# A macaron of two feed-forward blocks, attention and experts on one core: norms by half, an earlier table request, keys turned first

## What is computed

```python
x = x + 0.5 * _L0_ffn_ref(_layernorm(x), ...)   # step 1
x = x + _L0_attn_ref(_layernorm(x), ...)
x = x + 0.5 * _L0_ffn_ref(_layernorm(x), ...)   # step 3
x = x + 0.5 * experts(...); x = x + linear_attention(...); x = x + 0.5 * experts(...)

def _layer(x, wqkv, qs, ksc, wo, lg, lb, w1, b1, w2, b2):   # _L0_ffn_ref runs two of these
    q, k, v = split(shift_token(x) @ wqkv)          # 8 heads of 64
    q = q / clip(norm(q), 1e-12) * qs               # the same for k
    q, k = rotary_xpos(q, k)                        # q*cos*scale + rotate_half(q)*sin*scale; k with 1/scale
    x = x + local_attention(q, k, v) @ wo           # windows of 64, this one and the one before
    h = layernorm(shift_token(x)) * lg + lb
    a, g = split(h @ w1 + b1)                       # 341 each
    return x + (a * gelu(g)) @ w2 + b2
```

## Time and profile before

| | us |
|---|---|
| median of 3 executions | 2468.88 (2466.38 to 2472.57) |
| the profiled execution, its own time | 2465.03 |
| its span, first to last instruction | 2462.9 |
| PE, DVE, ACT, POOL busy | 2116.9, 1809.3, 1462.6, 1058.3 |
| mean granted TensorE clock | 0.946 of full speed |

### The profile page before, as it was taken

One profiled execution on the slowest core, in us unless ns is written; L12 is line 12 of the kernel. 1 busy time (PEld: TensorE's weight loads), 2 busy tenths in 40 slices (PEclk: granted clock), 3 DMA queues, 4 the chain that ended last, 5 costly groups with the idle time before them and its releaser, 6 DMA issues. The chain is left out here.

```text
span 2462.9 us, 56322 instructions
## 1 busy us (share of the span) xinstructions
PE 2116.9 (86%) x23398; PEld 1565.7 (64%) x23398; DVE 1809.3 (73%) x2815; ACT 1462.6 (59%) x2389; POOL 1058.3 (43%) x800
## 2 busy tenths in 40 slices
PE   2799999998989868999868999999989997597968
PEld 1566666666666645555536667676666664495758
DVE  3688888888888646777727888888888884563556
ACT  0477776766666515666546776766666674363635
POOL 4665555545555210000035565655555450550245
PEclk8799999999999968999979999999999998698979
DMA  7000000079999995000000000000000003121122
GB/s 151 1 2 1 2 2 2 1 78 105 111 137 129 126 127 51 2 2 2 2 1 1 2 2 2 2 2 2 2 2 2 1 2 76 54 66 37 35 75 80
DMA packets 211376, 90.91 MB, mean 37 GB/s; under 512 B 79700, under 2 KB 206721, under 8 KB 210996
## 3 DMA queue, kind: packets, MB, share of 16 engines
q1 hardware_dynamic: 202596, 72.27, 24.5%
q0 software_dynamic: 6080, 11.76, 1.5%
q10 hardware_dynamic: 2448, 3.28, 0.6%
HBM read 24.31 MB, written 63.41 MB: 36 GB/s over the span
## 5 line engine op out<-in xcount | busy, mean ns | idle before, releaser
L490 POOL TENSOR_TENSOR work<-work,rot_tables 128x512 f32<-128x512 f32 x256 | 382.6, 1515 | 317.3 <-ACT work L594 317.3
L498 POOL TENSOR_TENSOR work<-work 128x1024 f32<-128x1024 f32 x128 | 304.8, 2381 | 283.6 <-DVE work L924 278.4
L941 DVE TENSOR_TENSOR work<-work,small 128x1024 f32<-128x1024 f32 x128 | 234.4, 1833 | 56.6 <-ACT small L608 50.1
L924 DVE TENSOR_TENSOR work<-work,rot_tables 128x1024 f32<-128x1024 f32 x128 | 219.3, 1713 | 11.6 <-ACT work L594 11.6
L1081 DVE TENSOR_REDUCE small<-psum 128x4 f32<-128x1024 f32 x128 | 156.6, 1223 | 90.3 <-PE psum L1582 88.5
L1482 PE MATMUL psum<-centered,ffn_w 128*128 128x256 f32 x768 | 191.2, 401 | 3.0 <-DVE centered L985 2.9
L705 ACT ACTIVATE work<-psum 128x1024 f32<-128x1024 f32 x128 | 131.0, 1024 | 88.7 <-PE psum L1582 88.4
L1323 PE MATMUL psum<-qkv_w_hi,h_hi 128*128 128x512 f32 x384 | 180.0, 469 | 2.2 <-ACT work L594 2.2
L1420 PE MATMUL psum<-work 64*128 64x128 f32 (+1 forms) x2048 | 178.9, 304 | 0.0
L1482 PEld LDWEIGHTS psum<-centered,ffn_w 128*128 128x128 f32 x768 | 146.0, 197 | 31.2 <-DVE centered L985 4.4
L1453 PE MATMUL psum<-work,v 128*32 128x192 f32 (+1 forms) x4096 | 164.8, 302 | 0.0
(11 more groups left out here) (279 smaller groups left out, 5266.1 us busy)
## 6 DMA issues: line engine op xcount, KB each, us to landing
h_area<-mean_weights SPq DMA_DIRECT2D x24, 2048.0 KB
tile_x<-h_area SPq DMA_DIRECT2D x39, 128.5 KB, 2.1
stage<-in_consts ACTq DMA_DIRECT2D x1, 2817.0 KB, 12.0
tile_x<-h_area SPq DMA_DIRECT2D x39, 64.5 KB, 1.8
work<-in_x SPq DMA_DIRECT2D x4, 512.0 KB, 27.2
expert_w<-in_ew SPq DMA_DIRECT2D x1, 2048.0 KB, 8.4
expert_w<-in_ew SPq DMA_DIRECT2D x8, 256.0 KB, 6.6
work<-y_tokens SPq DMA_DIRECT2D x4, 512.0 KB, 6.1
```

What stands on the lines that cost most here:

```text
L490: last = pool.tensor_tensor(b[:, :, :, o_], a[:, :, :, i_], tab[:, l, 1, t, :, o_].unsqueeze(2).to_broadcast([P, 2, HEADS, 32]), ALU.mult)
L498: pool.tensor_tensor(rC[:, t, :], rC[:, t, :], rB[:, t, :], ALU.add).then_inc(f_sum, 1)
L924: dve.tensor_tensor(g(rC[:, t, :]), g(rA[:, t, :]), tab[:, l, 0, t, :, :].unsqueeze(2).to_broadcast([P, 2, HEADS, DH]), ALU.mult)\
L941: dve.tensor_tensor(c_, c_, sm[0][:, 96 + 16 * t:112 + 16 * t].unsqueeze(2).to_broadcast([P, 16, DH]), ALU.mult).then_inc(f_nrm, 1)
```

## The change

1. GpSimd's `rotated` becomes two instructions of 512 columns.
2. `clip`, `rnorm` are done for each tile by itself (16 columns each), and `qk_norm(i, 0)` waits only for tile 0's root.
3. On ACT the GELU table is asked for right behind `rstd`; `rnorm(i, 0)` comes behind `gelu`, then the exponentials, then `x_square` and `rnorm(i, 1)`.
4. On DVE `clip(i, 0)` comes behind `sums(i, 0)`, then `gated`, and only then `cosines(i, 1)`, `qk_norm(i, 0)`, `x_center`, `sums(i, 1)`, `clip(i, 1)`, `resid2`, `qk_norm(i, 1)`.
5. On PE the keys of both tiles are turned before any query; the wait for `o_norm` stands behind the keys.

```diff
                 def rotated(i, t):
...
-                    pool.tensor_tensor(rC[:, t, :], rC[:, t, :], rB[:, t, :], ALU.add).then_inc(f_sum, 1)
+                    for h in range(2):
+                        n_ = slice(h * INNER, (h + 1) * INNER)
+                        last = pool.tensor_tensor(rC[:, t, n_], rC[:, t, n_], rB[:, t, n_], ALU.add)
+                    last.then_inc(f_sum, 1)
...
-                def rnorm(i):
-                    act.wait_ge(f_ssm, i + 1)
-                    link(act.activation(sm[0][:, 64:96], sm[0][:, 32:64], ACT.Ln, scale=65536.0))
-                    act.activation(sm[0][:, 96:128], sm[0][:, 64:96], ACT.Exp, scale=-0.5, bias=half_ln[:, 0:1])\
-                        .then_inc(f_rn, 1)
+                def rnorm(i, t):
+                    part_ = lambda a: sm[0][:, a + 16 * t:a + 16 * t + 16]
+                    act.wait_ge(f_ssm, 2 * i + t + 1)
+                    link(act.activation(part_(64), part_(32), ACT.Ln, scale=65536.0))
+                    act.activation(part_(96), part_(64), ACT.Exp, scale=-0.5, bias=half_ln[:, 0:1]).then_inc(f_rn, 1)
...
                     if old:
                         square(i - 2)
                         rstd(i - 2)
+                        act.preload_act_table_set(GELU_SET)
...
                     if old:
                         gelu(i - 2)
+                    if new:
+                        rnorm(i, 0)
+                    if mid:
+                        for q in range(3):
+                            exps(i - 1, q)
                     if pre:
                         x_square(n)
                     if new:
-                        rnorm(i)
-                    if mid:
-                        for q in range(3):
-                            exps(i - 1, q)
+                        rnorm(i, 1)
...
-                def clip(i):
-                    dve.wait_ge(f_ss, 2 * i + 2)
-                    dve.tensor_scalar(sm[0][:, 32:64], sm[0][:, 0:32], 1e-24, None, ALU.max).then_inc(f_ssm, 1)
+                def clip(i, t):
+                    dve.wait_ge(f_ss, 2 * i + t + 1)
+                    dve.tensor_scalar(sm[0][:, 32 + 16 * t:48 + 16 * t], sm[0][:, 16 * t:16 * t + 16], 1e-24, None, ALU.max)\
+                        .then_inc(f_ssm, 1)
 
                 def qk_norm(i, t):
-                    dve.wait_ge(f_rn, i + 1)
+                    dve.wait_ge(f_rn, 2 * i + t + 1)
...
                     if new:
                         sums(i, 0)
-                        cosines(i, 1)
+                        clip(i, 0)
                     if old:
                         gated(i - 2)
                     if new:
-                        sums(i, 1)
-                        clip(i)
+                        cosines(i, 1)
+                        qk_norm(i, 0)
                     if pre:
                         x_center(n)
                     if new:
-                        qk_norm(i, 0)
+                        sums(i, 1)
+                        clip(i, 1)
...
                         last = turned(5, t, INNER)
-                        if t == TILES - 1:
-                            last.then_inc(f_kT, 1)
-                        else:
-                            free(pe, f_on, 2 * i - 1)
+                    last.then_inc(f_kT, 1)
+                    free(pe, f_on, 2 * i - 1)
+                    for t in range(TILES):
                         last = turned(3, t, 0)
                     last.then_inc(f_qT, 1)
```

More of the change, by code:

```diff
@@ L63 @@
 LN_SET = "natural_log_exp_and_others"
+GELU_SET = "gelu_and_others"
 def halves_of(a):
```

## The result

The changed kernel takes 2502.43 us (median of 4 executions, 2500.84 to 2515.59) against 2467.63 for the kernel before beside it (4 executions, 2466.15 to 2472.57): ratio 1.0137, 95% interval 1.0119 to 1.0156, slower. The forecast was 2462, its range 2430 to 2476: the time went up by 1.4%, where it was to stay or fall, and lies above the range. The profiled execution took 2502.99, its span is 2501.0, 38.1 longer than before, and the mean granted clock is 0.935 instead of 0.946.

The account below looks back on a forecast made before the run. DVE's line of work was taken to set the step's end, with PE close behind. Terms -1.7 - 4.5 + 4.8 - 5.6 = -7.0 us took 2465.03 to 2458.0, plus 3.85 for the median: 2461.9, range 2430 to 2476.

Parts of the forecast that it names:

- So all that PE gained in attention turns into a longer wait in `qk_T`: At the step's end, `attend` ends 1.1 earlier but `o_norm` starts at 424.27 (before 424.16), so PE waits for it.
- the wait of `down` for `x_center`: On PE in steps with the preparation: wait over 1 us, `down` starting 0.15 later, each step losing 0.20.
- the last sentence: Sign of failure on PE: the sum fails as a whole if the granted clock falls in the longer idle; no size.
- Q and W steps: 8 plain steps (Q) gain 0.21 each, 28 steps that also write into x (W) gain 0.16 each.
- P steps: 24 steps preparing the first layer norm: `down` waits for the later `x_center`, each loses 0.20 (bounds 0 and 0.4).
- POOL's halves: POOL's addition in two instructions: 2.35 and one more start, bounds 0 and 0.3, ending about 415.13.
- Keys first: In PE's turning, 16 turnings instead of 24 remain behind `o_norm`: 0.64 instead of 0.96.
- Start: Steps k = 0 and 1: early exponentials shorten PE's wait of 3.87; gain 2.8 a block, bounds 0 and 5.
- Clip loses its turn: On DVE, `clip(i, 1)` waits for POOL's second half, ends at 422.13 and is about 1.2 us long.
- Rival 1: `clip(i, 1)` slips in between POOL's halves; plain steps gain 0.80, steps writing into x 0.94: 2435.4, chance 0.17.
- Rival 2: POOL's half addition (1.15) goes ahead of `qk_norm(i, 0)`, delaying `x_center` and `down` in 24 steps: 2490, chance 0.10.
- Rivals 3 to 5: `copy_v` late, 2468 to 2480, chance 0.06; square reloads tables, about 2616, 0.03; drain with the load, 2522, 0.01.

Follow-up runs that it names:

- a1: The changed kernel with unread matrix products filling PE's two long waits (before `down`, and between tile 0's and tile 1's keys): 2471.04 us, ratio 1.0007.
- b1: The changed kernel with POOL's addition as one instruction of 1024 columns again: 2467.04 us, ratio 0.9977.
- a4: The kernel before with only the keys of both tiles turned ahead of any query: 2460.64 us, ratio 0.9961.
- d4: The changed kernel with tile 0's queries turned ahead of tile 1's keys again: 2530.29 us, ratio 1.0250.
- a3: The changed kernel without DVE's clip, the floor added as a bias in ACT's logarithm: 2464.89 us, ratio 0.9980.
- b2: The changed kernel without the early request for the GELU table: 2499.68 us, ratio 1.0117.
- d2: The changed kernel with one unread product in each long PE wait (before `down`, between the tiles' keys), none in plain steps: 2479.72 us, ratio 1.0036.
- each repair alone: The changed kernel with `x_center` moved right behind `gated` (2492.54 us), or with DVE's clip replaced by a bias in the logarithm (2464.89 us).
- both together: The changed kernel with `x_center` right behind `gated` and DVE's clip replaced by the logarithm's bias: 2418.36 us, ratio 0.9771.

## Why the prediction was wrong

- **The failed step: "So all that PE gained in attention turns into a longer wait in `qk_T`", priced at nothing**, and in the same way the wait of `down` for `x_center`, of which only the 0.20 of lateness was counted. The waits came where and as long as the text had them (over 1 us before `down`: 1.74; before the queries 1.1 and 2.0 in Q and W: 0.92 + 0.26 and 1.72 + 0.26). What they do to the clock was named in the last sentence as what would break the sum, but had no term, no rival and no chance. It is 33.4 of the 38.1 us. a1, with the waits filled, shows it: 2471.04, 9 above the forecast. The other terms, -7.0 in the text, came to +4.7. Of this second miss of 12, 7 are Q and W steps, 2 the start, 1 the P steps and 1 the stretch behind block 2.
- **POOL's halves, priced at one more start of 0 to 0.3.** The start was right: 2.51 against 2.35. What it does further down the line was missed: in b1 a Q step is 0.29 shorter, W 0.25 and P 0.14. With the clock the halves cost 35 by the medians, 44 by the marks of the two blocks.
- **Q and W steps, -0.21 and -0.16 predicted, +0.06 and +0.04 measured.** Mis-sized by 0.2 to 0.3. From the cosines of tile 0 to `o_norm` it took 13.20 in the Q step at 440.84 (13.14 in the one before), where 12.97 was predicted and 12.86 was before. Of the 0.23, 0.11 are there when the second cosines end: two sines took 2.50, not 2.34, and two halves of the addition 2.51, not 2.47. `qk_norm(i, 1)` took 1.28 in that step (1.23 in the one before), where 1.23 was taken.
- **P steps, +0.20 predicted, 24.48 - 24.24 = +0.24 measured.** Right, by the way foretold: `x_center` behind cosines and `qk_norm(i, 0)`. (The text's "96.4 us less far on" is a slip: its own times, 416.21 and 319.28, are 96.9 apart, and the sum goes by those.)
- **Keys first** was taken as part of the Q and W terms. Alone it is worth 0.22 to 0.26 a step (a4), and much more where a long idle would stand in one piece (d4, 28 us).
- **Start, -5.6 predicted, -3.4 measured** (-1.5 and -1.9 in the stretches that hold it), inside its bounds. The fall in block 1's step k = 1 takes 1.6 of it away.
- **Clip loses its turn**: right, 1.25. Rival 1 is out. Its mirror, a3, says what it would have been worth: 0.73 in Q, 0.64 in W, not 0.80 and 0.94.
- **Rival 2** had nearly the time (2490), not the mechanism: `qk_norm(i, 0)` started 0.07 to 0.09 before the cosines' end, ahead of POOL's addition, in 62 of 64 steps (the two others are k = 0). **Rivals 3 to 5** are out: no wait of PE for `v`, two loads a step, and the activation after the moved load starts 0.01 behind its end (167.58 + 1.28, 168.87). The Trainium skill, "ScalarE: Activation LUTs", section "What ACT_TABLE_LOAD costs", adds a drain to the load; this trace shows none, as before.

**Open.** Why the clock falls in one step and not in the next is not settled. In P steps of the changed kernel the same idle of 1.71 to 1.74 is followed by a fall in 7 of 24, and in W steps of b2 the idle of the changed kernel in 7 of 26 instead of 15. Filling or shortening the idle of one kernel took falls away each time (a1, d2, b1), but its length doesn't order the kernels: 2.5 in W of d4 gives 17 lengthened steps of 26, 1.7 to 1.8 gives 7 to 17, 1.5 in b1 one, 1.1 in d2 and 1.0 in a3 four each, and 1.0 in W steps of the kernel before none; nor do the 8 Q steps of d4, with 1.56 to 1.64, have one. All idle of a step taken together doesn't order them either: by the windows above PE was not busy for 2.2 in a W step before (313.25 - 284.51, by 13) and for 2.0 in the changed kernel. No run here isolates what else counts.

## What to carry over

Where PE is the busiest engine, don't price a longer wait of it at nothing because the step's end doesn't move: gather all of its idle by size, before and after, and give the case that the granted clock falls a term of its own (here 22 falls of 1.5 us). An edit that joins small waits into one long one is suspect even where it shortens the work, as here in W steps, where PE's idle fell from 2.2 to 2.0 and the clock was lost all the same. Unread products in the wait tell in one run whether the clock is the price. And when two late lines end together, repair both before judging either: here each repair alone gave P steps 0.3 or nothing, and both together 1.53.

## What the runs showed of the hardware

- The granted clock fell to 0.51 with PE 86% busy over the span, behind single idle stretches of 1.72 to 1.80 that came once in a step of 24 us; in W steps of a3 and d2 stretches of 1.0 to 1.2 preceded a few falls. In one W step PE resumed at 701.01 with the full clock (1.00 up to 702.60), and the low level (0.50) showed behind that, in `proj`. At the low clock six products of `down` took 2.88 instead of 1.53, and the eight of `proj` 2.99 instead of 1.89; each fall made a step 1.2 to 1.7 longer.
- Products that nobody reads, 1.56 us of them in a P step's wait, made the kernel 31 us faster.
- A DVE instruction of 16 columns took 1.25, since it waited for a POOL instruction of 512 columns under way; and halving POOL's instruction gave DVE no turn in between, while the pair became 0.16 us longer (2.51 against 2.35).
